# Down projections and the 128x128 product of a linear-attention block split in high and low parts; output tiles scaled by ScalarE and added by GpSimd

## What is computed

```python
x = x + attn_a(layernorm(x), ...)   # linear attention, 16 heads, elu + 1
x = x + ffn(layernorm(x), ...)      # _sq_relu(xf @ Ws1) @ Ws2, plus routed experts
x = x + attn_b(layernorm(x), ...)   # only the first 16 tokens of a sequence get attention
x = x + ffn(layernorm(x), ...)
```

## Time and profile before

| | |
|---|---|
| median of 3 runs | 457.89 us (457.2 to 458.69) |
| profiled execution: its time | 457.29 us |
| its span | 455.5 us |
| PE busy | 425.2 us (93%) |
| DVE busy | 293.2 us (64%) |
| POOL busy | 203.5 us (45%) |
| ACT busy | 183.8 us (40%) |
| mean granted clock of PE | 0.993 of full speed |
| DMA | 20.58 MB, 45 GB/s in the mean |

### The profile page before, as it was taken

The page is one execution under the profiler, slowest core; times in us unless marked ns, Lnnn a source line. Parts: engine busy times, 40 slices in busy tenths (PEclk is TensorE's granted clock), DMA queues, the critical chain, the costliest instruction groups (busy, mean ns, idle before and its releaser), DMA issues.

```text
span 455.5 us, 7618 instructions
## 1 busy us (share of the span) xinstructions
PE 425.2 (93%) x2570; PEld 354.7 (78%) x2570; DVE 293.2 (64%) x651; ACT 183.8 (40%) x321; POOL 203.5 (45%) x334
## 2 busy tenths in 40 slices
PE   7799989999999999688979999999999999999971
PEld 4689979998898999676858876878777787787851
DVE  4565575455556543459637697878858777887843
ACT  2464545555455541224134532333243323424440
POOL 3344442433334350036144367566527527635562
PEclk9999999999999999999999999999999999999997
DMA  8512111111100003100110111011010111011102
GB/s 260 179 48 78 63 47 46 48 46 46 46 0 1 0 2 89 8 2 3 51 46 4 50 49 35 15 48 47 4 47 1 50 48 35 16 49 47 48 32 71
DMA packets 22776, 20.58 MB, mean 45 GB/s; under 512 B 3255, under 2 KB 22717, under 8 KB 22717
## 3 DMA queue, kind: packets, MB, share of 16 engines
q1 hardware_dynamic: 22156, 19.32, 13.5%
q10 hardware_dynamic: 560, 0.52, 0.4%
HBM read 11.32 MB, written 8.45 MB: 43 GB/s over the span
## 4 chain that ended last, share of the span: by engine, by line
PE 82%; DVE 7%; ACT 5%; issue 2%; POOL 2%; DMA 1%; POOLq 0%; ACTq 0%; DVEq 0%
PE PG L1236 11%; PE PB L1356 6%; PE PT L1395 6%; PE PA L1356 5%; PE PB L1377 5%; PE PA L1425 4%; PE PA L1431 3%; PE PA L1426 3%; PE PA L1226 3%; PE PA L1227 3%; PE PA L1228 3%; PE PB L1214 3%; PE PB L1212 3%; PE PB L1213 3%; PE PT L1435 3%; PE PA L1367 3%
## 5 line engine op out<-in xcount | busy, mean ns | idle before, releaser
L454 POOL TENSOR_TENSOR ln_a<-ln_bn 128x4 f32<-128x4 f32 x32 | 6.5, 205 | 132.0 <-DVE ln_bn L934 132.0
L1236 PE MATMUL PG<-scratch 128*128 128x256 f32 x256 | 58.0, 379 | 1.3 <-DVE scratch L821 1.3
L821 DVE SCALAR_TENSOR_TENSOR scratch<-scratch,PB 128x1024 f32<-128x1024 f32 x16 | 19.5, 1221 | 60.3 <-ACT scratch L570 60.3
L1236 PEld LDWEIGHTS PG<-scratch 128*128 128x128 f32 x256 | 47.4, 190 | 7.4 <-issue 1.5
L535 ACT ACTIVATE scratch<-x_all,ln_shift,ln_rstd 128x255 f32 (+1 forms) x60 | 31.1, 589 | 36.7 <-PE PG L1236 30.2
L934 DVE BATCH_NORM_STATS2 ln_bn<-x_all 128x6 f32<-128x256 f32 x128 | 44.9, 413 | 0.9
L416 POOL TENSOR_SCALAR ln_rstd<-ln_mv 128x4 f32<-128x4 f32 x16 | 3.7, 228 | 91.3 <-DVE ln_mv L743 88.4
L1212 PE MATMUL PB<-wk_hi,xt_hi 128*128 128x256 f32 x128 | 39.0, 305 | 0.4 <-DVE xt_lo L768 0.4
L429 POOL TENSOR_TENSOR x_all<-x_all,scratch 128x1024 f32 (+1 forms) x16 | 38.2, 2388 | 0.6 <-ACT scratch L535 0.5
L429 POOL TENSOR_TENSOR x_all<-x_all,ob_rows 128x1024 f32<-128x1024 f32 x16 | 37.8, 2360 | 0.0
L695 ACT ACTIVATE scratch<-PA,ln_rsq 128x256 f32<-128x256 f32 x32 | 13.4, 471 | 59.3 <-PE PA L1356 35.4
(11 more groups left out here) (239 smaller groups left out, 1039.0 us busy)
## 6 DMA issues: line engine op xcount, KB each, us to landing
out_dram<-x_all SPq DMA_DIRECT2D x16, 512.0 KB, 3.1
x_all<-n_L_attn_a_inputs_q_dram SPq DMA_DIRECT2D x15, 512.0 KB, 3.6
x_all<-n_L_attn_a_inputs_q_dram ACTq DMA_DIRECT2D x2, 128.0 KB, 2.8
x_all<-n_L_attn_a_inputs_q_dram SPq DMA_DIRECT2D x2, 128.0 KB, 2.6
scratch<-in_L_attn_a_Wk_dram SPq DMA_DIRECT2D x1, 256.0 KB, 4.6
scratch<-in_L_attn_a_Wq_dram ACTq DMA_DIRECT2D x1, 256.0 KB, 5.0
scratch<-in_L_attn_a_Wv_dram SPq DMA_DIRECT2D x1, 256.0 KB, 6.8
scratch<-in_L_attn_a_Wo_dram SPq DMA_DIRECT2D x1, 256.0 KB, 6.2
```

The lines of the kernel that those rows point to most:

```text
L1236: last = mm(PG[:, c, 0:D], k_tok[:, t, c * P:(c + 1) * P], xn[g % 2][:, t, :], start=(g == 0 and t == 0), stop=(g == G - 1 and t == T - 1))
```

## The change

Four things are changed.

1. `down` and the wc product work on high and low parts. `ws2` and `wc` are split once, in step 0 (two ACT copies, two DVE subtractions). For h2 and h3, ACT squares twice, once into the float32r tile (`h2_hi`, `h3_hi`) and once in place, and POOL subtracts (`h2_low`, `h3_low`: 128x512 each). Each `down` is 12 matmuls where it was 4 float32 ones, and wc is 3 where it was 1.
2. DVE multiplies h2 by half the reciprocal standard deviation before the square, where it multiplied the square by the reciprocal variance. The r2 transposes move ahead of OT on PE.
3. The output of group v: ACT scales all four tiles, POOL adds all of them in one 128x1024 instruction, DVE none. DVE computes the reciprocal variances of group v from POOL's variances (`reciprocal_variances`), between its `reciprocal` of the norms and its multiplications of O. Its `bn3` statistics move ahead of chain slot 3.
4. POOL's order in a step changes: `h3_low` first, both output and h2_low after `add_row`, and the chain's slot 1 behind them. Several semaphores of the chain are merged, and tiles are laid out anew in SBUF.

The core of the diff (left out: the layout of tiles, the renamed semaphores of the chain, the splitting of `ws2` and `wc` in step 0, the moved `bn3` statistics, the lines where r2 stood on PE):

```diff
--- before.py
+++ after.py
@@ -459,8 +479,22 @@
                 nc.gpsimd.tensor_tensor(d, d, d, ALU.mult).then_inc(powed, 1)
                 pool.wait_ge(powed, 5 * j + 4)
                 nc.gpsimd.tensor_tensor(a, a, d, ALU.add).then_inc(powed, 1)
-                pool.wait_ge(powed, 5 * j + 5)
-                nc.gpsimd.tensor_tensor(ln_rsq[:, slot, :], a, minus_ones[:, :], ALU.pow).then_inc(done, 1)
+
+            def half_rstd2(r):
+                ge(pool, r2_mm, r)
+                four_variances(0, r, bn2, pow2)
+                pool.wait_ge(pow2, 5 * r + 5)
+                nc.gpsimd.tensor_tensor(ln_rsq[:, 0, :], ln_a[:, 0, :], minus_half[:, 0:T], ALU.pow).then_inc(rsq2, 1)
+
+            def h2_low(r):
+                pool.wait_ge(f1_sq, r + 1)
+                ge(pool, f2_mm, r)
+                nc.gpsimd.tensor_tensor(h2_lo[:, :], h2, h2_hi[:, :].bitcast(F32), ALU.subtract).then_inc(h2_lo_done, 1)
+
+            def h3_low(v):
+                pool.wait_ge(f3_sq, v + 1)
+                ge(pool, f4_mm, v)
+                nc.gpsimd.tensor_tensor(h3_lo[:, :], h3, h3_hi[:, :].bitcast(F32), ALU.subtract).then_inc(h3_lo_done, 1)
...
@@ -500,21 +534,25 @@
                 i = g * B + b
                 r, nr, _ = lagged(g, b, 1)
                 v, nv, _ = lagged(g, b, 2)
+                if runs(v):
+                    h3_low(v)
                 if runs(r):
-                    ge(pool, r2_mm, r)
-                    rsq(0, r, bn2, pow2, rsq2)
+                    half_rstd2(r)
                 if runs(v):
-                    ge(pool, out_dve, 2 * v)
-                    ge(pool, f4_scaled, 2 * v)
-                    rsq(1, v, bn3, pow3, rsq3)
+                    ge(pool, rsq3, v)
+                    four_variances(1, v, bn3, pow3)
                 if runs(r):
                     pool.wait_ge(t2_mm, C * (r + 1))
                     add_row(nr, ob_rows, ob_added)
+                if runs(v):
+                    pool.wait_ge(f4_scaled, T * (v + 1))
+                    if v < B:
+                        pool.wait_ge(c_xs, 16 * (v + 1))
+                    last = x_all[:, nv * T:(nv + 1) * T, :]
+                    nc.gpsimd.tensor_tensor(last, last, y3[:, :, :], ALU.add).then_inc(out_pool, 1)
+                if runs(r):
+                    h2_low(r)
                 chain(i, 1)
-                if runs(v):
-                    pool.wait_ge(f4_scaled, 2 * (v + 1))
-                    last = x_all[:, nv * T + 2:(nv + 1) * T, :]
-                    nc.gpsimd.tensor_tensor(last, last, y3, ALU.add).then_inc(out_pool, 1)
                 chain(i, 2)
                 if runs(r):
                     run_experts(r)
...
@@ -691,8 +731,8 @@
                     act.wait_ge(f4_mm, v + 1)
                     act.wait_ge(rsq3, v + 1)
                     ge(act, out_pool, v)
-                    for t in range(2, T):
-                        nc.scalar.activation(y3[:, t - 2:t - 1, :], four(PA)[:, t:t + 1, :], ACT.Copy,
+                    for t in range(T):
+                        nc.scalar.activation(y3[:, t:t + 1, :], four(PA)[:, t:t + 1, :], ACT.Copy,
                                              scale=ln_rsq[:, 1, t:t + 1]).then_inc(f4_scaled, 1)
                 chain(i, 1)
                 if runs(i):
@@ -702,17 +742,23 @@
                         nc.scalar.activation(o_hi[:, c, :], PB[:, c, :], ACT.Copy).then_inc(o_hi_done, 1)
                 if runs(r):
                     act.wait_ge(f1_mm, r + 1)
-                    ge(act, f1_scaled, r)
+                    ge(act, h2_lo_done, r)
                     nc.scalar.activation(h2, PT[:, 0, :], ACT.Relu, scale=2.0).then_inc(f1_relu, 1)
-                    act.wait_ge(f1_relu, r + 1)
+                    act.wait_ge(f1_scaled, r + 1)
+                    ge(act, f2_mm, r)
+                    nc.scalar.activation(h2_hi[:, :], h2, ACT.Square).then_inc(h2_hi_done, 1)
+                    act.wait_ge(h2_hi_done, r + 1)
                     nc.scalar.activation(h2, h2, ACT.Square).then_inc(f1_sq, 1)
                 chain(i, 2)
                 if runs(r):
                     run_experts(r)
                     act.wait_ge(f3_mm, r + 1)
-                    ge(act, f4_mm, r)
+                    ge(act, h3_lo_done, r)
                     nc.scalar.activation(h3, PT[:, 0, :], ACT.Relu, scale=2.0, bias=w1ob[:, 0:1]).then_inc(f3_relu, 1)
                     act.wait_ge(f3_relu, r + 1)
+                    ge(act, f4_mm, r)
+                    nc.scalar.activation(h3_hi[:, :], h3, ACT.Square).then_inc(h3_hi_done, 1)
+                    act.wait_ge(h3_hi_done, r + 1)
                     nc.scalar.activation(h3, h3, ACT.Square).then_inc(f3_sq, 1)
                 chain(i, 3)
 
...
@@ -932,6 +978,11 @@
             def x_stats(n, slot, bn):
                 for t in range(T):
                     nc.vector.bn_stats(ln_bn[:, slot, t:t + 1, :], x_tile(n, t)).then_inc(bn, 1)
+
+            def reciprocal_variances(v):
+                dve.wait_ge(pow3, 5 * (v + 1))
+                ge(dve, f4_scaled, T * v)
+                nc.vector.reciprocal(ln_rsq[:, 1, :], ln_a[:, 1, :]).then_inc(rsq3, 1)
 
             def step(g, b):
                 i, n, _ = lagged(g, b, 0)
@@ -947,6 +998,8 @@
                     last.then_inc(o_norm, 1)
                     dve.wait_ge(o_norm, 2 * i + 1)
                     nc.vector.reciprocal(norm_inv[:, :, :], norm_sb[:, :, :]).then_inc(o_norm, 1)
+                    if runs(v):
+                        reciprocal_variances(v)
                     dve.wait_ge(o_norm, 2 * i + 2)
                     ge(dve, ot_mm, C * i)
                     for k0, nb, reg in regions:
@@ -954,20 +1007,16 @@
                                                 reg.rearrange("p (k w) -> p k w", w=KVW)[:, :, 0:P].rearrange("p k (h e) -> p k h e", e=HD),
                                                 norm_inv[:, k0:k0 + nb, :].unsqueeze(3).to_broadcast([P, nb, HC, HD]),
                                                 ALU.mult).then_inc(o_done, 1)
+                elif runs(v):
+                    reciprocal_variances(v)
                 if i == 0:
                     batch_kv(B - 1)
                     dve.wait_ge(fold_sb, 1)
                     nc.vector.scalar_tensor_tensor(w1c, colsum.rearrange("p (o f) -> p o f", o=1).to_broadcast([P, C, F]), -1.0 / D,
                                                    ws1[:, :, :], ALU.mult, ALU.add).then_inc(w1c_ready, 1)
-                if runs(v):
-
-                    dve.wait_ge(f4_mm, v + 1)
-                    dve.wait_ge(rsq3, v + 1)
-                    if v < B:
-                        dve.wait_ge(c_xs, 16 * (v + 1))
-                    for t in range(2):
-                        nc.vector.scalar_tensor_tensor(x_tile(nv, t), four(PA)[:, t:t + 1, :], ln_rsq[:, 1, t:t + 1], x_tile(nv, t),
-                                                       ALU.mult, ALU.add).then_inc(out_dve, 1)
+                    for k, (lo, whole, hi) in enumerate(((ws2_lo, ws2[:, :], ws2_hi), (wc_lo, wc, wc_hi))):
+                        dve.wait_ge(ffn_hi, k + 1)
+                        nc.vector.tensor_tensor(lo[:, :], whole, hi[:, :].bitcast(F32), ALU.subtract).then_inc(ffn_lo, 1)
                 chain(i, 1)
                 if runs(i):
 
@@ -978,10 +1027,9 @@
                                                 ALU.subtract).then_inc(o_lo_done, 1)
                 if runs(r):
 
-                    dve.wait_ge(f1_sq, r + 1)
+                    dve.wait_ge(f1_relu, r + 1)
                     dve.wait_ge(r2_mm, r + 1)
-                    ge(dve, f2_mm, r)
-                    nc.vector.tensor_tensor(h2s, h2, PT[:, 1, :], ALU.mult).then_inc(f1_scaled, 1)
+                    nc.vector.tensor_tensor(h2, h2, PT[:, 1, :], ALU.mult).then_inc(f1_scaled, 1)
                 chain(i, 2)
                 if runs(i):
 
...
@@ -1351,9 +1400,12 @@
                     last = mm(PA[:, 1, C * P:(C + 1) * P], w1c[:, c, :], ob_t[:, c, :], start=(c == 0), stop=(c == C - 1))
                 last.then_inc(fold_mm, 1)
 
-            def down(pair, h, done):
+            def down(pair, hi, lo, done):
                 for t in range(T):
-                    last = mm(four(pair)[:, t, :], h[:, t * P:(t + 1) * P], ws2[:, :], start=True, stop=True)
+                    dst, tile = four(pair)[:, t, :], slice(t * P, (t + 1) * P)
+                    mm(dst, hi[:, tile], ws2_hi[:, :], start=True, stop=False)
+                    mm(dst, hi[:, tile], ws2_lo[:, :], start=False, stop=False)
+                    last = mm(dst, lo[:, tile], ws2_hi[:, :], start=False, stop=True)
                 last.then_inc(done, 1)
 
             def step(g, b):
@@ -1382,18 +1434,26 @@
                     g_transposes(B - 1)
                     kv_product(B - 1)
                 if runs(v):
-                    pe.wait_ge(f3_sq, v + 1)
+                    pe.wait_ge(h3_lo_done, v + 1)
                     pe.wait_ge(t2_done, min(C * (r + 1), C * NG))
```

(19 more changed lines are left out.)

199 lines of the change are left out of this document (106 added, 93 removed).

## The result

| | before | after |
|---|---|---|
| median | 458.29 us (457.2 to 458.75, 4 runs) | 475.06 us (474.46 to 476.5, 4 runs) |
| ratio | | 1.0374, 95% interval 1.0342 to 1.0406 |
| span of the profiled execution | 455.5 us | 472.8 us |
| mean granted clock | 0.993 | 0.984 |

A forecast was written before the change was run, and what follows sets the result against it. PE was taken to bound the kernel, other chains within a few tenths. Its terms (4.4 + 7.2 - 1.7 + 2.6 + 2.9 + 0.5) gave 15.9 on 457.29, so 473.2; moved to the median, 473.5 us, range 463 to 482.

The forecast's parts named there:

- PE's own work: PE's matmuls in each step: down 1.44 us for 1.72, wc 0.72 for 0.86, in all 0.70 us a step saved.
- B: Part of a step from O to OT, 4.94 us before; POOL's new first instruction and DVE's reciprocal there: +7.2 in sum.
- The wait for h2_lo, +4.4: PE stalls about 0.72 us at wc's third matmul for POOL's subtraction: plus 0.30 in each of steps 1 to 15.
- A: Part of a step from the end of W to the first O product that waits for `f2_added`, 4.06 us before.
- one wait only: Rival: of the added waits in A and B only one stays, the other falls away; 466 us, chance 0.20.
- Step 5, +2.6: DVE's slot (5, 2) instruction waits for a small POOL power behind h2_lo: +2.6 once, beyond A's 0.3.
- r2, -1.7 in C: The r2 transposes' 0.44 us leaves C, which gets 0.43 shorter in steps 8, 11, 13 and 14: -1.7.
- C: Part of a step from OT to W, 1.84 us before.
- Output, nothing within the pipeline: DVE's two fewer instructions, ACT's four scaled tiles and POOL's sum of 2.39 for 1.28 cost nothing within the pipeline.
- The third rival: POOL's large sums and DVE's chain instructions block each other in about five steps, up to 2 us each: 481, chance 0.17.
- D: Part of a step from W to its end, 2.96 us for 24 high/low matmuls before.
- The tail, +2.9: Step 16, where no W covers anything: later third wc matmul +1.9, variances about -0.8, ACT +0.84, POOL's sum +1.1; together +2.9.

The follow-up runs named there:

- experiment 1: The changed kernel, but PE's third wc product and the down projections out of PB take h2_hi for h2_lo and don't wait for it: 467.04 us, 1.0222.
- experiment 5: The changed kernel with the r2 transposes back behind the OT transposes: 472.40 us, 1.0321.
- experiment 6: The changed kernel with its output part undone (two tiles by DVE, two scaled by ACT and added by POOL in one 128x512 sum): 469.44 us, 1.0279.
- experiment 8: The changed kernel with POOL's 128x1024 output sum cut into two of 128x512: 474.51 us, 1.0377.
- experiment 3: The kernel of experiment 1 with POOL's subtraction of h2_lo also taken out, h3_lo kept: 457.85 us, 1.0024.
- experiment 4: The changed kernel with the h2_lo subtraction moved from POOL to DVE, nothing left out of the result: 461.92 us, 1.0091.
- experiment 7: The kernel before with the output part alone (ACT scales four tiles, POOL adds them in one 128x1024 sum), no split: 465.03 us, 1.0176.
- experiment 11: The kernel of experiment 9 with the h3_lo subtraction back on POOL, at the head of its step: 458.13 us, 1.0012.
- experiment 2: The kernel of experiment 1 with both POOL subtractions, h2_lo and h3_lo, gone and down out of PA taking h3_hi twice: 455.18 us, 0.9941.
- experiment 9: The changed kernel with both subtractions on DVE, POOL back to two powers to -1, h2 squared before its copy, r2 behind OT, output halved: 456.51 us, 0.9966.

## Why the prediction was right, and where it wasn't

*PE's own work*: right. A down of 1.44, three wc products of 0.23 each when nothing waits, and with the low parts' waits gone B is 5.07 against the 5.09 worked out.

*The wait for h2_lo, +4.4*: the mechanism is right, and experiment 1 takes it away. The size was too big (2.9), since it isn't in 15 steps. In 8 and 11 (chain work in slot 2) and in 2 (W late, by the lower clock) h2_lo is ready before PE comes to it, and PE's shorter down then shows: A is 0.45 below the kernel before. With step 2 at the full clock, as in experiments 5 and 6, it would be 3.9.

*B, +7.2*: the size was near (5.7, of it 0.7 of the output's), the cause only in part. The forecast built B's end on h3's chain starting after A's stall, then put all of B's wait down to h3_lo and the variances behind it. Experiment 1, with POOL's program untouched, takes B of 2, 5 and 15 from 5.58 to 5.17 or 5.18, PE's own 5.07 and 0.1; taking h3_lo away on top brings 0.07 to 0.09 there. So the wait for h2_lo, seen a second time, is enough to explain most of B's excess in these steps. Both delays lie on one chain, and how much taking out h3_lo alone would have brought is open: no run leaves the wait for h2_lo in and takes h3_lo out. Step 8's +1.31 (+2.0 forecast) was h2_lo's place, as the forecast had it: 5.92 without PE's wait, 5.13 without the subtraction. The rival "one wait only" let one wait fall and the other stay; experiment 1 takes away the first and most of the second.

*Step 5, +2.6*: the mechanism is right, and the size within 0.7. A of step 5 is 4.53 before, 7.83 changed, 6.70 with the same waits at the full clock (experiment 8), 6.73 without PE's wait and 4.07 without POOL's subtraction. The wait is thus 1.9 beyond A's 0.3; that 3.0 was measured is the lower clock of this execution, 1.1.

*r2, -1.7 in C*: right, -1.6, and its cost in B was confirmed, 0.43 or 0.44 a step for 0.44.

*Output, nothing within the pipeline*: wrong. This is the step of the forecast that failed. It looked only at whether POOL was free again ahead of h2_lo and ACT ahead of o_hi, not at who runs beside POOL's sum or which chain work stands behind ACT's tiles. Undone, it gives back 4.4 us, and in the profiled execution 2.6 within steps 1 to 15, 0.5 of that the clock of step 2; alone, it costs 3.0 there, with no fall of the clock in these steps. The third rival had the mechanism, with a price of up to 2 us in five steps. It showed in C of step 2 and D of step 7, added to the other terms and not instead of them. B of step 3 (0.72) is no collision but the forecast's other "nothing", ACT's two more tiles: ACT's small chain copy stands behind its scaling, 1.57 us now and 0.84 before, and PE's 16 small products wait for that copy, 1.89 us and not 1.17. The line of before, then that of the changed kernel:

```profile
232.91 2.02 PE L1473 MATMUL PG<-q_all,b_weights 128*128 128x128 f32 x16 [1.17 <-ACT q_all L631]
```

```profile
236.33 2.02 PE L1530 MATMUL PG<-q_all,b_weights 128*128 128x128 f32 x16 [1.89 <-ACT q_all L669]
```

On the collisions the Trainium skill (SBUF — State Buffer, "SBUF: two separate sides") says that whoever comes second is blocked for the whole instruction. The trace agrees: DVE's 64x256 products of two SBUF tiles end 0.28 us after POOL's sum whether they took 1.27, 1.73 or 2.47 us, and take 0.42 with no sum beside them.

*The tail, +2.9*: short by 1.1. PE waits 2.43 and 1.31 us in step 16 and then runs at a lower clock: granted 0.52 from 458.4 to 461.0, where the down into PB takes 0.21 a product, 2.6 us for 1.44.

```profile
457.83 0.80 PE L1492 MATMUL PT<-h_lo,wc_hi 128*128 128x512 f32 x1 [1.31 <-POOL h_lo L492]
458.42 0.42 PE L1406 MATMUL PB<-ws_hi,h_hi 128*128 128x256 f32 x1
458.63 0.42 PE L1407 MATMUL PB<-ws_lo,h_hi 128*128 128x256 f32 x1
```

*The lower clock in steps 2 and 5, some 1.6*: in no term. So that 15.9 came near 17.3 is partly luck: A and B were 2.6 too high, C, D, the tail and the start 4.0 too low, and the clock's share isn't the program's alone.

## What to carry to other kernels

A 1.3 us operation put at the end of a queue that is half idle cost 16 us (experiment 3), since PE, a small instruction behind it and the next group's work on the same queue all waited for it; on the busier engine, in a gap where that engine waited anyway, the same operation cost 3 us (experiment 4). Place an added operation by the gap of the engine and what stands behind it, not by the engine's busy share. When two forecast waits lie on one chain, the later one must be worked out again with the first taken away, before both are summed. And of an operation that grows on POOL, list DVE's instructions on SBUF tiles that start within its span; of one that grows on any engine, list what stands behind it in that engine's order. Before the parts of two profiles are subtracted, the granted clock of each part must be looked at: here it alone made 1.1 us of step 5 and 1.3 of step 7.

## What the runs showed of the hardware

- DVE's block beside POOL isn't only for two SBUF tensors: a TENSOR_SCALAR of 64x256 took 2.25 us beside POOL's 128x1024 sum (experiment 7) and ended 0.15 us after it; the same instruction took 0.35 in the changed kernel with no sum beside it. The Trainium skill (SBUF — State Buffer, "Who interferes with whom") counts tensor_scalar among the operations that can use the shared ports; the trace agrees. DVE's 128x1024 sums with a PSUM operand and its statistics never showed it: 1.20 to 1.23 us and 0.39 to 0.43 us each, in six profiles.
- Pieces of a POOL sum that follow each other directly let DVE in only sometimes (step 7 of experiment 8, not its step 2).
- The granted clock within steps 1 to 15 isn't fixed by the program's waits. After PE had waited 2.66 us in step 2 of the changed kernel it was 0.67 in the mean from 219.00 to 223.40, a mixture of 1.2 and 2.4 GHz: W's products stood 0.21 apart until 221.97 and 0.12 after that. Experiments 1, 3 and 4 have the same wait of 2.65 us there and kept the full clock. In step 5 it is the changed kernel against experiment 8, waits of 0.75 and 1.22 us in both. Nine of the thirteen profiles have such a stretch in these steps; the kernel before and experiments 3, 4 and 7 have none.
- The clock also differs between executions where the programs don't: in 20 to 40 us it was 1.00 in nine profiles (the kernel before and the changed one among them) and 0.91 in four (experiments 1, 4, 7 and 11), in which step 1's O began at 196.9 to 197.3 against 195.4 and 195.7 in those two. In three more (experiments 2, 5 and 9) it fell near 187 us, and O began at 196.3 to 196.5. A difference of that size between two profiles is no evidence; sums of parts are, once each part's clock has been compared.
